# Second LoRA factors of a two-layer adapted FFN: spread over the partitions by small on-chip copies instead of through DRAM

## The reference, cut to what matters

```python
# layer 0
c0 = einsum('bsi,boi->bso', x, W0[itok_B_3_7])           # a 512x512 matrix per batch
lo = einsum('bsr,bor->bso', einsum('bsd,brd->bsr', c0, A[adapter0]), B[adapter0])   # rank 16
x1 = x + einsum('bsd,od->bso', c0, W1) + bias1 + where(use_lora, lo, 0)
# layer 1
c1 = x1 @ W2.T + bias2 + scale[b] * (x1 @ A1[id].T @ B1[id].T)                      # rank 16
H  = c1 @ W3.T + b3;  z = c1 @ A
# the routing weights come from H[:, :8], z and LiMEs at every second token,
# scaled by two maxima over all batches, a softmax and a soft top 2
out = x1 + H + einsum('btr,ro->bto', z * p_mix, Bmat) * 0.5
```

## Time and profile before

| | |
|---|---|
| time, median of 3 runs | 135.06 us (134.25 to 137.37) |
| profiled execution: its time / its span | 134.48 us / 132.5 us |
| busy share of the span: PE, DVE, ACT, POOL | 91%, 63%, 43%, 17% |
| mean granted TensorE clock | 0.974 |
| moved by DMA | 23.04 MB; HBM read 18.64 MB, written 4.29 MB |

### The profile page before, as it was taken

One profiled execution on the slowest core, in us unless ns is written; L12 is line 12 of the kernel. 1 busy time (PEld: TensorE's weight loads), 2 busy tenths in 40 slices (PEclk: granted clock), 3 DMA queues, 4 the chain that ended last, 5 costly groups with the idle time before them and its releaser, 6 DMA issues.

```text
span 132.5 us, 1890 instructions
## 1 busy us (share of the span) xinstructions
PE 120.9 (91%) x703; PEld 103.3 (78%) x703; DVE 83.6 (63%) x172; ACT 56.5 (43%) x94; POOL 22.5 (17%) x30
## 2 busy tenths in 40 slices
PE   6999999999829999999818999999989999999992
PEld 2488777888719999998717898999978878688891
DVE  0599299848967496754299376087995557431671
ACT  3374499459977374905914613153051011031000
POOL 3077815040047505000041000000000000000000
PEclk9999999999995999999997799999999999999999
DMA  3999965999389993896980000000000000000673
GB/s 108 383 393 413 404 251 140 332 398 327 95 357 380 294 329 101 287 376 203 409 326 4 0 0 0 5 0 0 0 0 0 5 0 0 0 0 0 227 272 137
DMA packets 7752, 23.04 MB, mean 174 GB/s; under 512 B 800, under 2 KB 1184, under 8 KB 7488
## 3 DMA queue, kind: packets, MB, share of 16 engines
q1 hardware_dynamic: 4784, 13.06, 26.7%
q0 software_dynamic: 2624, 9.44, 20.3%
q10 hardware_dynamic: 336, 0.44, 0.9%
HBM read 18.64 MB, written 4.29 MB: 173 GB/s over the span
## 4 chain that ended last, share of the span: by engine, by line
PE 59%; DMA 15%; DVE 15%; issue 4%; ACT 3%; SPq 1%; ACTq 0%; DVEq 0%
PE bank L851 45%; DMA b_rows<-c_lo 7%; DVE w_lo L542 5%; DMA x_in<-in_x 5%; DMA b<-b_rows 4%; PE bank L963 3%; PE bank L953 3%; DVE c_row L747 2%; PE bank L956 2%; PE bank L959 2%; DVE m_lo L581 2%; PE bank L888 1%; DVE bm_parts L740 1%; DVE x_lo L533 1%; ACT w_hi L381 1%
## 5 line engine op out<-in xcount | busy, mean ns | idle before, releaser
L336 POOL DMA_INDIRECT w_in<-in_W,rows_i x16 | 16.8, 1048 | 30.4 <-DVE w_lo L542 12.5
L851 PE MATMUL bank<-c_hi,w_hi 128*128 128x256 f32 x64 | 18.8, 294 | 2.9 <-DMA b<-b_rows 2.9
L542 DVE TENSOR_TENSOR w_lo<-w_in,w_hi 128x1024 fp32r<-128x1024 f32 x16 | 19.1, 1220 | 2.8 <-ACT w_hi L381 2.7
L851 PE MATMUL bank<-c_lo,w_hi 128*128 128x256 f32 x64 | 18.8, 294 | 0.0
L851 PE MATMUL bank<-c_hi,w_lo 128*128 128x256 f32 x64 | 18.8, 294 | 0.0
L381 ACT CAST w_hi<-w_in 128x1024 fp32r<-128x1024 f32 x16 | 16.1, 1047 | 3.5 <-DMA w_in<-in_W,rows_i 3.5
L851 PE MATMUL bank<-w_hi,x_hi 128*128 128x512 f32 x32 | 13.7, 428 | 3.1 <-issue 2.9
L851 PEld LDWEIGHTS bank<-c_hi,w_hi 128*128 128x128 f32 x64 | 12.8, 200 | 3.2 <-issue 3.0
L851 PE MATMUL bank<-m_hi,x_hi 128*128 128x512 f32 (+1 forms) x36 | 13.8, 385 | 0.0
L851 PE MATMUL bank<-m_hi,x_lo 128*128 128x512 f32 (+1 forms) x36 | 13.2, 367 | 0.0
L851 PE MATMUL bank<-w_hi,x_lo 128*128 128x512 f32 x32 | 13.2, 413 | 0.0
(11 more groups left out here) (181 smaller groups left out, 241.9 us busy)
## 6 DMA issues: line engine op xcount, KB each, us to landing
w_in<-in_W SPq DMA_DIRECT2D x5, 512.0 KB, 4.9
x_in<-in_x SPq DMA_DIRECT2D x4, 512.0 KB, 7.3
out_dram<-w_in SPq DMA_DIRECT2D x7, 256.0 KB, 3.0
be<-be_rows SPq DMA_DIRECT2D x1, 1120.0 KB, 5.1
b<-b_rows SPq DMA_DIRECT2D x1, 1024.0 KB, 4.7
w_in<-in_W SPq DMA_DIRECT2D x1, 1024.0 KB, 9.1
be_rows<-low_t SPq DMA_DIRECT2D x1, 840.0 KB, 5.2
b_rows<-c_lo SPq DMA_DIRECT2D x1, 768.0 KB, 4.6
```

The lines of the kernel that those rows point to most:

```text
L336: nc.gpsimd.indirect_dma_start(w_in[:, slot, half * h:half * (h + 1)], None, W0, row).then_inc(w_landed[b][h], 16)
L542: nc.vector.tensor_tensor(part(w_lo[:, b % 2], h), raw(b, h), f32(part(w_hi[:, b % 2], h)), ALU.subtract).then_inc(w_lo_done, 1)
L851: ins = mm(o, st, mv, start=start and n == 0, stop=stop and n == len(parts) - 1)
```

## The change

The DRAM tensors are gone. For each pair and each of the four groups, SP issues one transfer from SBUF to SBUF of 32 partitions (512 columns for b0, 560 for be): 16 for b0 and 16 for be. For that the partitions are ordered (pair, row), on the host and in `bits`, and `turn_rows` writes plainly. x of pair 2 is issued between the copies of b0's pairs 1 and 2, x of pair 3 after those of pair 3 and `a1_ready`. W1 no longer waits for `g0_landed`, x of pair 2 no longer for W0 of batch 3. The last parts of be (`bes_hi`, `bes_done`) are made earlier in ACT's and DVE's order, those of bm before `x1_high(2, 1)` and `x1_low(2, 1)`. `layer_b(i, 0)` waits for b0 of its pair, DVE waits for all of b0 before it writes `c0_low(2)`, and `low1_high(0)` waits until be has landed.

```diff
             slot, half = w_slot("w1"), C * D // 2
-
-            sp.wait_ge(g0_landed, 16)
             sp.wait_ge(w2_lo_done, 4)
             sp.wait_ge(w3_lo_done, 4)
...
-            def spread(parts, rows, stored):
-
-                src = f32(parts[:, 0]).unsqueeze(1).to_broadcast([P, G - 1, parts.shape[-1]])
-                sp.dma_start(rows[0:G - 1].rearrange("g p d -> p g d"), src).then_inc(stored, 16)
-                sp.dma_start(rows[G - 1], f32(parts[:, 1])).then_inc(stored, 16)
-
-            def gathered(rows):
-                return rows.rearrange("g (k i) d -> (g k) (i d)", i=NP)
+            def spread(t, parts, i, landed):
+
+                for g in range(G):
+                    sp.dma_start(f32(t[K2 * g:K2 * (g + 1), i]),
+                                 f32(parts[K2 * i:K2 * (i + 1), 0 if g < G - 1 else 1])).then_inc(landed, 16)
 
             sp.wait_ge(b0_hi_done, 1)
             sp.wait_ge(b0_done, 1)
-            spread(b0_parts, b0_rows, b0_stored)
-            sp.wait_ge(b0_stored, 32)
-            sp.dma_start(f32(flat(b0[:])), gathered(b0_rows)).then_inc(b0_landed, 16)
+            spread(b0, b0_parts, 0, b0_landed[0])
+            spread(b0, b0_parts, 1, b0_landed[1])
             sp.wait_ge(a0_ready, 1)
-            sp.wait_ge(w_landed[3][1], 16)
             load_x(2)
+            spread(b0, b0_parts, 2, b0_landed[2])
+            spread(b0, b0_parts, 3, b0_landed[3])
+            sp.wait_ge(a1_ready, 1)
+            load_x(3)
             sp.wait_ge(be_hi_done, 1)
             sp.wait_ge(be_done, 1)
             sp.wait_ge(bes_hi_done, 1)
             sp.wait_ge(bes_done, 1)
-            spread(be_parts, be_rows, be_stored)
-            sp.wait_ge(a1_ready, 1)
-            load_x(3)
-            sp.wait_ge(be_stored, 32)
-            sp.dma_start(f32(flat(be[:])), gathered(be_rows)).then_inc(be_landed, 16)
+            for i in range(NP):
+                spread(be, be_parts, i, be_landed)
...
                 if i == 0:
-                    act.wait_ge(be_stored, 32)
+                    act.wait_ge(be_landed, 16 * NP * G)
...
             low0_high(0)
+            act.wait_ge(bes_summed, 1)
+            nc.scalar.copy(be_parts[:, 0, D:], bes_f[:]).then_inc(bes_hi_done, 1)
             w_high(3)
...
                 c0_high(2 * i + 1)
+                if i == NP - 1:
+                    act.wait_ge(late_landed, 16)
+                    nc.scalar.copy(bm_parts[:], bm4).then_inc(bm_hi_done, 1)
                 x1_high(i - 1, 1)
...
-                bits(1, 0, NP - 1)
-                bits(2, 2, RANK - 1)
-                bits(3, 6, 1)
+                bits(1, 5, NP - 1)
+                bits(2, 0, RANK - 1)
+                bits(3, 4, 1)
                 bits(4, 4, 1)
...
             low0_low(0)
+            dve.wait_ge(bes_hi_done, 1)
+            nc.vector.tensor_tensor(be_parts[:, 1, D:], bes_f[:], f32(be_parts[:, 0, D:]),
+                                    ALU.subtract).then_inc(bes_done, 1)
             w_low(3)
...
             x_low(2)
+            for i in range(NP):
+                dve.wait_ge(b0_landed[i], 16 * G)
             c0_low(2)
...
                 c0_low(2 * i + 1)
+                if i == NP - 1:
+                    dve.wait_ge(bm_hi_done, 1)
+                    for a in (1, 3):
+                        at = slice(R * a, R * (a + 1))
+                        nc.vector.tensor_tensor(bm_parts[at], bm4[at], f32(bm_parts[at]),
+                                                ALU.subtract).then_inc(bm_done, 1)
                 x1_low(i - 1, 1)
...
                     pe.wait_ge(be_done, 1)
-                    pe.wait_ge(b0_landed, 16)
                 else:
                     pe.wait_ge(a1_hi_done, 1)
                     pe.wait_ge(a1_done, 1)
+                if h == 0:
+                    pe.wait_ge(b0_landed[i], 16 * G)
...
-            pe.wait_ge(be_landed, 16)
+            pe.wait_ge(be_landed, 16 * NP * G)
```

More of the change, by code:

```diff
@@ L52, in place, with build @@
         at += w
-def build(nc, x, W0, W1, W23, g0, g1, scale, early, al, late, b0_rows, be_rows, out):
+def build(nc, x, W0, W1, W23, g0, g1, scale, early, al, late, out):
     ctx = ExitStack()
@@ L167, in build @@
         g0_landed, g1_landed, s_landed = sem("g0_landed"), sem("g1_landed"), sem("s_landed")
-        b0_stored, be_stored, w3_landed = sem("b0_stored"), sem("be_stored"), sem("w3_landed")
-        b0_landed, be_landed = sem("b0_landed"), sem("be_landed")
+        w3_landed = sem("w3_landed")
+        b0_landed, be_landed = [sem(f"b0_landed{i}") for i in range(NP)], sem("be_landed")
         late_landed = sem("late_landed")
@@ L490, in _ @@
             nc.scalar.copy(ae[:, :, 0:NS], ae_f[:]).then_inc(ae_hi_done, 1)
-            act.wait_ge(bes_summed, 1)
-            nc.scalar.copy(be_parts[:, 0, D:], bes_f[:]).then_inc(bes_hi_done, 1)
             for i in range(2, NP):
@@ L504, in _ @@
                 c0_high(2 * i + 1)
+                if i == NP - 1:
+                    act.wait_ge(late_landed, 16)
+                    nc.scalar.copy(bm_parts[:], bm4).then_inc(bm_hi_done, 1)
                 x1_high(i - 1, 1)
-            act.wait_ge(late_landed, 16)
-            nc.scalar.copy(bm_parts[:], bm4).then_inc(bm_hi_done, 1)
             low0_high(NP - 1)
@@ L714, in _ @@
             nc.vector.tensor_tensor(ae[:, :, NS:2 * NS], ae_f[:], f32(ae[:, :, 0:NS]), ALU.subtract).then_inc(ae_done, 1)
-            dve.wait_ge(bes_hi_done, 1)
-            nc.vector.tensor_tensor(be_parts[:, 1, D:], bes_f[:], f32(be_parts[:, 0, D:]),
-                                    ALU.subtract).then_inc(bes_done, 1)
             for i in range(2, NP):
@@ L736, in _ @@
             low1_low(NP - 2)
[L737 to L740, removed]
             dve.wait_ge(w3_landed, 16)
@@ L939, in layer_low1, with turn_rows @@
                 low_rank(bank[7][:, 0:2 * S], a1, i, x_hi[:, i], x_lo[:, i]).then_inc(low1_ready, 1)
-            def turn_rows(o, rows, by_pair):
+            def turn_rows(o, rows):
                 for c in range(C):
                     to = chunk(o[:], c)
-                    last = nc.tensor.transpose(to.rearrange("p (i k) -> p k i", k=K2) if by_pair else to, chunk(rows, c),
+                    last = nc.tensor.transpose(to, chunk(rows, c),
                                                ident[:])
@@ L981, in _ @@
             pe.wait_ge(ident_done, 1)
-            turn_rows(bank[7], rows1[:, D:2 * D], False).then_inc(b1_ready, 1)
+            turn_rows(bank[7], rows1[:, D:2 * D]).then_inc(b1_ready, 1)
             layer_a(0)
@@ L997, in _ @@
             pe.wait_ge(g0_landed, 16)
-            turn_rows(bank[6], rows0[:, 0:D], True).then_inc(a0_ready, 1)
+            turn_rows(bank[6], rows0[:, 0:D]).then_inc(a0_ready, 1)
             layer_a(1)
@@ L1011, in _ @@
                             [(small_parts[:, c], b2_parts[:, c]) for c in range(C)]).then_inc(smalls_ready, 1)
-                    turn_rows(bank[5], rows1[:, 0:D], True).then_inc(a1_ready, 1)
+                    turn_rows(bank[5], rows1[:, 0:D]).then_inc(a1_ready, 1)
                 layer_low0(i - 1)
@@ L1161 @@
     g0 = np.concatenate([np.zeros((RANK, 2 * D), np.float32), table(v["L0_ffn_lora_A"], v["L0_ffn_lora_B"])])
-    by_rank = np.broadcast_to(v["itok_B_1_7"].reshape(NP, 2).T[:, None, :], (2, RANK, NP))
+    by_rank = np.repeat(v["itok_B_1_7"], RANK)
     ids = np.concatenate([np.broadcast_to(v["itok_B_3_7"], (P, NB)), by_rank.reshape(P, 1),
@@ L1182 @@
         args.append(nc.dram_tensor("in_" + name, a.shape, mybir.dt.from_np(a.dtype), kind="ExternalInput").ap())
-    args.append(nc.dram_tensor("b0_rows", (G, K1, D), F32, kind="Internal").ap())
-    args.append(nc.dram_tensor("be_rows", (G, K1, D + NS), F32, kind="Internal").ap())
     args.append(nc.dram_tensor("out_dram", (NB, S, D), F32, kind="ExternalOutput").ap())
```

## The result

The changed kernel takes 129.1 us (median of 4 runs, 128.53 to 129.41), the kernel before 136.04 in the same comparison (134.25 to 137.37). The medians differ by 6.9 us. A run more than 1.5% above the fastest of its kernel counts as a slow one, two of the four runs before do (137.02 and 137.37), and the ratio of the others is 0.958, 95% interval 0.951 to 0.966: faster, by 5.6 us. The forecast was 124.1 with a range of 122.4 to 128.4, so the direction was right, the size was not, and the time lies above the range. The profiled execution has a span of 127.3 us, against 132.5.

What follows compares the result with a forecast made beforehand. The kernel was taken as PE-bound with two holes. Terms 5.1 + 5.6 + 0 - 0.2 = 10.5 gave 124.0 from the profiled 134.48 us, 124.6 from the median 135.06; it said 124.1, range 122.4 to 128.4.

Steps and rivals of the forecast that it cites:

- First hole: PE's idle time around the L0 low-rank product and `layer_b(0, 0)`: keeping b0 out of DRAM gains 5.1 us.
- The cost of a copy: SP's issue time for each on-chip copy of b0 and be: taken as 0.40 us, kept between 0.39 and 1.31.
- Landing: Time from issue until the b0 and be copies are in place: taken as 2 us, from output stores' 1.7 to 3.1.
- rival 3: be copies on SP's queue cost too much issue time; from 0.70 us each, `low1_high(0)` stalls, up to 145 us; chance 0.14.
- Loss of 0.2 us here: At `turn_c0(3)`: ACT ends `save_c0(3)` at 46.0, PE wants it at 45.9; a loss of 0.2 us booked.
- rival 1: Batch 4 weights land late beside be's copies; PE idles 3.0 us at `turn_c0(3)`, loses 4.4 with low clock: 128.4; chance 0.18.
- Second hole: PE's idle time before `layer_a(6)`: be without DRAM and x of pair 3 early gain 5.6 us.
- bm: Earlier bm subtractions remove PE's 0.62 us wait at 97.08 but cost 0.6 at `layer_low1(2)`: net 0, bounds -0.6 to +0.6.
- The low clock: PE's stretch at 1.2 instead of 2.4 GHz after a hole, booked at 1.57 us each.

## Why the prediction was wrong

**First hole: right.** "Gain 5.1 us": measured 4.64; 0.2 of the missing 0.5 is that this execution's PE is 0.2 us behind from before 21 us on (21.00 against 20.79 at the first `layer_a`). The low-rank product started at 35.65, and W1's low part was no obstacle. b0 had the cover that the prediction gave it, even at 0.75 us a copy. Two slips in the working change nothing: PE's idle time there is 40.02 - 37.00 = 3.02 us, not 2.97, and at 1.31 a copy pair 0 would be there at 33.3, not 33.4.

**The cost of a copy: the first step that failed.** "I take 0.40" was 0.68 to 0.75. The row nearest in shape was a single transfer from DRAM; the rows of issues that follow each other on a loaded queue went up to 1.31. With it the start of x of pair 3 was wrong: I let it go out "at about 35.5", when a1's turn is done. At 0.40 SP would have been free then, at 0.7 it was not, and x went out at 38.42.

**Landing: the second.** "Landing: ... I take 2", from output stores at the end of the kernel, when the queues are empty. be's copies took 7.3 us (median), beside 3 MB of weights. By the formula of rival 3 with t = 0.69, be should have been in place at 29 + 32 x 0.69 = 51; it was 57.8. Of the 6.8 us between, 5.7 are the landing (the last copy was issued at 50.13 and took 7.7 where I had 2) and 1.1 the later start (39.17, where the formula has 27 + 16 x 0.69 = 38.0). So the condition of that rival, "from t = 0.70", was wrong by its constant, and the rival was given 0.14 for what in part came true.

**"Loss of 0.2 us here": the third.** It was 2.67, from the end of PE's last matmul to the turn. I let the second half of batch 4 land after the 5.4 us of the earlier trace rows. It took 8.3, the very figure of rival 1 (8.4 from batch 6). Its mechanism was named and its price, 3.0 us of idle time, was near; I weighed it at 0.18 by comparing bytes in the queue (1.5 MB before, 1.1 MB after). The bytes were the wrong measure if a byte of these costs the engines 1.7 times as much or more, as the window above suggests; that this is why the weights were late is argued, not shown. That be's copies delay them is shown by the table above.

**Second hole: half right.** From the start of `layer_a(4)` to the end of `layer_a(6)` the kernel before took 74.33 - 51.38 = 22.95 us, the changed one 69.03 - 49.61 = 19.42. So "gain 5.6 us" was 3.53. Of the missing 2.07, 1.80 is the idle time that was left, by be's landing through ACT's and DVE's order.

**bm: right**, net 0, with 0.66 and 0.62 for my 0.6 and 0.62.

**The sum.** 4.64 - 2.87 + 3.53 = 5.30, where I had 5.1 - 0.2 + 5.6 = 10.5; 2.87 is how far the lead fell at the fourth turn (4.64 to 1.77). Rival 1 and a mild form of rival 3 came true together, each worth 2 to 3 us. The range treated them as alternatives, and its upper end of 128.4 (128.5 by its own terms, 3.0 + 1.57 - 0.2) held one of them alone. Both hang on be's copies, so they should have been added. The low clock, which rival 1 had priced at 1.57, did not come in the profiled execution.

## What to carry to other kernels

A copy on chip by many small transfers had three prices here: a time per transfer on the issuing queue that hardly depended on what was in it; more engine time for a byte, with 32 partitions at a time (1.7 times in the mixed window); and the delay of what was in the queues beside and behind it. Estimate landing times from rows of the same stretch, with the same neighbours in the queues, not from a quiet one. When a transfer can't be made sooner, look for who waits for it only because of a written order (`low1_high(0)` here): moving the waiter was worth 1.9 us for a few lines, and holding be back until the weights had landed another 2.8, by medians of different comparisons. Holding be back alone cost 5.4 and 6.3 us. And a stretch that runs slower in front of a wait can cost nothing, so compare where the last matmul stands before a difference in time is put down to it.

## What the runs showed of the hardware that was not expected

- An SBUF-to-SBUF transfer among others costs SP 0.61 to 0.84 us, as the mean of groups of 2 to 32, for 32 or 128 partitions and 35 to 280 KB. The groups of one kind spread as widely as the kinds do: b0's first eight took 0.63 to 0.84 in the different profiles. x of pair 3, 512 KB from DRAM, cost 0.58 right behind copies in the changed kernel and 0.33 after a pause of 5.6 us with full-width transfers (35.61 above).
- Idle time does not by itself set the low clock's stretch. The changed kernel stood 2.67 us before 49.2 and kept a granted clock of 1.00 (2.4 GHz) from 50 to 52, and so it did when it was run again, with 2.16 us. With W1 waiting again PE stood 2.35 us at nearly the same place and had 0.50 (1.2 GHz) there, and with low1 later 2.48 us, with 0.50. So the 1.57 us after each hole that I booked as part of the hole are not a fixed price.
- The landing of batch 4's second half differed between kernels whose programs are alike up to there: a wait of 1.06 us in one profiled execution and 2.16, 2.48 and 2.67 in three. A wait behind a loaded queue, read from one execution, is good to about a microsecond and a half here.
- The last output store, 128 KB, landed in 1.7 us in the changed kernel, 2.7 with be through DRAM and 3.0 with W1 waiting again, with no loads in the queues any more. That is up to 1.3 us of a kernel's time that no edit here touches.
